# Storing the edge features once and splitting them on TensorE, in a four-layer graph network

## The reference, cut to what matters

```
edge_emb = edge_attr @ W_edge + b_edge
msg = jax.nn.relu(node_feats[src] + edge_emb)
aggr = jax.ops.segment_sum(msg, dst, num_segments=N)
h = (1.0 + eps) * node_feats + aggr
```

## Time and profile before

| what | value |
|---|---|
| time, median of 3 runs (lowest to highest) | 3059.01 us (3057.54 to 3060.01) |
| profiled execution, first to last instruction | 2795.5 us |
| mean granted TensorE clock | 0.952 |
| PE busy, share of the span | 2528.3 us, 90% |
| DVE busy | 2138.1 us, 76% |
| ACT busy | 1682.1 us, 60% |
| POOL busy | 1299.1 us, 46% |
| DMA moved | 338.46 MB |

### The profile page before, as it was taken

One profiled execution on the slowest core, in us unless ns is written; L12 is line 12 of the kernel. 1 busy time (PEld: TensorE's weight loads), 2 busy tenths in 40 slices (PEclk: granted clock), 3 DMA queues, 4 the chain that ended last, 5 costly groups with the idle time before them and its releaser, 6 DMA issues. The chain is left out here.

```text
span 2795.5 us, 45377 instructions
## 1 busy us (share of the span) xinstructions
PE 2528.3 (90%) x13039; PEld 1993.9 (71%) x13039; DVE 2138.1 (76%) x4172; ACT 1682.1 (60%) x3746; POOL 1299.1 (46%) x1279
## 2 busy tenths in 40 slices
PE   6999899999799999879899989598999999987887
PEld 4598555554488999648799984366888888765766
DVE  9699899998537888553588874866999999866667
ACT  1299888872226777413477761324888888845560
POOL 1777000007305677640377667315777777710211
PEclk9999999999899999998999999899999999988999
DMA  2210000013344453324455447225888888840201
GB/s 90 78 40 3 13 0 0 0 43 123 124 179 121 145 147 112 124 76 158 112 149 140 146 107 91 98 89 188 276 276 278 274 273 278 232 104 32 78 1 45
DMA packets 126768, 338.46 MB, mean 121 GB/s; under 512 B 25255, under 2 KB 39530, under 8 KB 126638
## 3 DMA queue, kind: packets, MB, share of 16 engines
q0 software_dynamic: 60768, 172.88, 22.0%
q1 hardware_dynamic: 65870, 163.93, 18.0%
HBM read 243.04 MB, written 85.82 MB: 118 GB/s over the span
## 5 line engine op out<-in xcount | busy, mean ns | idle before, releaser
L1839 POOL DMA_INDIRECT x_got<-table_dram,src_idx x376 | 418.8, 1114 | 117.3 <-issue 99.3
L722 POOL DMA_INDIRECT feature_rows<-in_edge_attr,ids x376 | 367.4, 977 | 117.4 <-issue 110.1
L1969 DVE TENSOR_TENSOR msg<-bank,x_got 128x512 f32<-128x512 f32 x376 | 252.7, 683 | 73.6 <-PE bank L1864 53.5
L1278 DVE TENSOR_TENSOR pt_low<-bank,pt_high 128x640 fp32r<-128x640 f32 x320 | 262.8, 822 | 54.9 <-ACT pt_high L1241 53.4
L673 ACT ACTIVATE hot_rest<-hot_dst,slot_w 128x128 bf16<-128x128 bf16 x864 | 272.6, 399 | 38.4 <-DVE hot_dst L633 38.4
L1241 ACT CAST pt_high<-bank 128x640 fp32r<-128x640 f32 x320 | 219.9, 688 | 117.6 <-PE bank L1192 117.4
L725 POOL COPY ids<-id_idx 128x136 uint32<-128x136 uint32 (+2 forms) x5 | 1.2, 242 | 612.5 <-DVE id_idx L840 347.6
L1918 ACT ACTIVATE msg_high<-msg 128x512 fp32r<-128x512 f32 x329 | 206.8, 628 | 74.8 <-DVE msg L1969 74.8
L1272 DVE CUSTOM_DVE_ANT_0 p<-bank,log_counts 128x1254 f32<-128x1254 f32 x160 | 232.6, 1454 | 13.7 <-PE bank L1175 13.6
L1192 PE MATMUL bank<-ident,p 128*128 128x128 f32 x1600 | 229.1, 275 | 2.3 <-DVE pt_low L1278 2.3
L1949 DVE SCALAR_TENSOR_TENSOR msg_low<-msg,msg_high 128x512 fp32r<-128x512 f32 x329 | 223.7, 680 | 0.0
(11 more groups left out here) (408 smaller groups left out, 6687.9 us busy)
## 6 DMA issues: line engine op xcount, KB each, us to landing
features_dram<-feature_parts POOLq DMA_DIRECT2D x94, 512.0 KB, 3.0
edge_got<-features_dram SPq DMA_DIRECT2D x94, 512.0 KB, 4.9
qk_dram<-qk_high SPq DMA_DIRECT2D x16, 640.0 KB, 2.9
qk_dram<-qk_low SPq DMA_DIRECT2D x16, 640.0 KB, 4.2
keys<-qk_dram SPq DMA_DIRECT2D x32, 320.0 KB, 4.7
queries<-qk_dram SPq DMA_DIRECT2D x32, 320.0 KB, 6.7
queries_low<-qk_dram SPq DMA_DIRECT2D x32, 320.0 KB, 8.9
acc_a<-zeros SPq DMA_DIRECT2D x1, 6400.0 KB, 30.6
```

Source lines behind the costliest of these rows:

```text
L722: pool.indirect_dma_start(out=rows[:, g % 2, j * ED:(j + 1) * ED], out_offset=None, in_=self.a.edge_attr_128, in_offset=bass.IndirectOffse ...
L1278: dve.tensor_tensor(p_low[:, made % 3, :, columns], unit(2 * n + u).rearrange("p (j n) -> p j n", n=P), p_high[:, made % 3, :, columns].bi ...
L1839: pool.indirect_dma_start(out=xg[:, g % XRING, j, :], out_offset=None, in_=k.table_dram, in_offset=bass.IndirectOffsetOnAxis(ap=k.src_idx[ ...
L1969: dve.tensor_tensor(msg[:, j, :], k.bank[:, 2 + j, :], xg[:, r, j, :], ALU.add).then_inc(added_x, 1)
```

## The change

The features are stored whole. POOL only gathers and saves: the float32r copy, the subtraction and `parts` are gone, the save (now 256 KB) goes straight out of `rows[:, u]`, and therefore the gathers of group g+1 now stand behind the wait for the save of group g-1, whose buffer they overwrite.

In `edge_messages`, PE turns four whole float32 tiles in transpose mode into one bank (bank 0 for even groups, 1 for odd). ACT copies the bank to float32r, which is the high part. PE then adds a product of minus the identity with that high part into the same bank (`take_off`), which leaves the low part there, and ACT copies the bank a second time. So the split of a group is a chain turn, high copy, `take_off`, low copy. PE does `take_off` behind the following `embed`; ACT does the high copy early, right behind the first rectification and the one-hot matrix of group g, and the low copy behind all of them.

```diff
@@ Features.gather @@
         for g in range(first, first + groups):
             u = g % 2
+            if g > first:
+                gate(pool, self.saved, of(16 * g, 16 * LAYER_GROUPS), self.passed)
             if g + 1 < first + groups:
                 load(g + 1)
             gate(pool, self.got[u], of(16 * GT * (g // 2 + 1), 16 * GT * LAYER_GROUPS // 2), self.passed)
-            if g > first:
-                gate(pool, self.saved, of(16 * g, 16 * LAYER_GROUPS), self.passed)
-            pool.tensor_copy(parts[:, 0, :], rows[:, u, :]).then_inc(self.made, 1)
-            gate(pool, self.made, of(2 * g + 1, 2 * LAYER_GROUPS), self.passed)
-            pool.tensor_tensor(parts[:, 1, :], rows[:, u, :], parts[:, 0, :].bitcast(F32), ALU.subtract).then_inc(self.made, 1)
-            gate(pool, self.made, of(2 * g + 2, 2 * LAYER_GROUPS), self.passed)
-            pool.dma_start(k.features_dram[bass.ds(of(g, LAYER_GROUPS), 1), :, :].rearrange("g p n -> (g p) n"),
-                           parts[:].rearrange("p q n -> p (q n)").bitcast(F32)).then_inc(self.saved, 16)
+            pool.dma_start(k.features_dram[bass.ds(of(g, LAYER_GROUPS), 1), :, :].rearrange("g p n -> (g p) n"), rows[:, u, :]).then_inc(self.saved, 16)
@@ layer2 @@
-            dve.tensor_copy(messages.ident_r[:], k.ident[:]).then_inc(messages.w_split, 1)
+            dve.tensor_scalar(messages.minus_r[:], k.ident[:], -1.0, None, ALU.mult).then_inc(messages.w_split, 1)
@@ edge_messages, PE @@
                 if not first:
-                    pe.wait_ge(e_copied, (i * 2 + u) * 2)
+                    pe.wait_ge(e_low, i * 2 + u - 1)
                 pe.wait_ge(got_e[u], i * 16 + 16)
-                for q in range(2):
-                    for j in range(GT):
-                        t = pe.matmul(k.bank[:, q, j * P:(j + 1) * P], ea[:, u, q, j, :], ident_r[:], start=True, stop=True)
-                    t.then_inc(turned_e, 1)
+                for j in range(GT):
+                    t = pe.matmul(k.bank[:, u, j * P:(j + 1) * P], ea[:, u, j, :], k.ident[:], is_transpose=True, start=(j == 0), stop=False,
+                                  skip_group_check=True)
+                t.then_inc(turned_e, 1)
+
+            def take_off(i, u):
+                pe.wait_ge(e_high, i * 2 + u + 1)
+                pe.matmul(k.bank[:, u, :], minus_r[:], et[:, u, 0, :], start=False, stop=True, skip_group_check=True).then_inc(e_rest, 1)
@@ the loop of pairs @@
                 turn(i + 1, 0)
                 embed(i, 1)
+                take_off(i + 1, 0)
                 collect(i, 0)
                 turn(i + 1, 1)
                 embed(i + 1, 0)
+                take_off(i + 1, 1)
                 collect(i, 1)
@@ edge_messages, ACT @@
                     if j == 0:
                         act.wait_ge(apart, g * GT + GT)
                         act.activation(hot[:, u], distance[:, u], ACT.Relu, bias=one[:], scale=-1.0).then_inc(hot_ready, 1)
+                        if following:
+                            copy_high(*following)
...
-                relu(i, 0)
-                copy_turned(i + 1, 0)
-                relu(i, 1)
-                copy_turned(i + 1, 1)
+                relu(i, 0, following=(i + 1, 0))
+                copy_low(i + 1, 0)
+                relu(i, 1, following=(i + 1, 1))
+                copy_low(i + 1, 1)
```

More of the change, by code:

```diff
@@ L704, in __init__ @@
         self.k, self.a = k, a
-        self.staged, self.made, self.passed = S("ids_staged"), S("parts_made"), S("features_passed")
+        self.staged, self.passed = S("ids_staged"), S("features_passed")
         self.got, self.saved = [S(f"features_got{u}") for u in range(2)], S("features_saved")
@@ L710, in places @@
         self.rows = r.take("feature_rows" + where, [P, 2, GT * ED], F32)
-        self.parts = r.take("feature_parts" + where, [P, 2, GT * ED], F32R)
     def gather(self, pool, first, groups, turn, l=None):
-        k, ids, rows, parts = self.k, self.ids, self.rows, self.parts
+        k, ids, rows = self.k, self.ids, self.rows
         def of(n, a_layer):
@@ L1530, in message_weights @@
     r = Region(nc, k.tail - 4 * KC * NP, k.tail)
[L1531 removed]
+    m.ea = r.take("edge_got", [P, 2, GT, ED], F32)
     m.we = r.take("w_edge", [ED, D], F32)
     m.w_high, m.w_low = r.take("w_edge_high", [ED, D], F32R), r.take("w_edge_low", [ED, D], F32R)
[L1534 removed]
+    m.minus_r = r.take("minus_ident_r", [P, P], F32R)
     m.one, m.one_eps = r.take("one", [P, 1], F32), r.take("one_eps", [P, 1], F32)
@@ L1813, in edge_messages @@
     xg = r.take("x_got", [P, XRING, GT, D], F32)
-    ea, w_high, w_low, ident_r, one = messages.ea, messages.w_high, messages.w_low, messages.ident_r, messages.one
+    ea, w_high, w_low, minus_r, one = messages.ea, messages.w_high, messages.w_low, messages.minus_r, messages.one
     et = r.take("edge_turned", [P, 2, 2, GT * P], F32R)
@@ L1882, in _ @@
             turn(0, 0, True)
-            turn(0, 1)
+            take_off(0, 0)
+            turn(0, 1, True)
+            take_off(0, 1)
             embed(0, 0)
@@ L1897, in _, with copy_high @@
         def _(act):
-            def copy_turned(i, u, first=False):
+            def copy_high(i, u, first=False):
                 g = i * 2 + u
@@ L1902, in copy_turned, with copy_low, relu @@
                     act.wait_ge(emb_done, (g - 1) * GT)
-                for q in range(2):
-                    act.wait_ge(turned_e, g * 2 + q + 1)
-                    act.copy(et[:, u, q, :], k.bank[:, q, :]).then_inc(e_copied, 1)
+                act.wait_ge(turned_e, g + 1)
+                act.copy(et[:, u, 0, :], k.bank[:, u, :]).then_inc(e_high, 1)
+            def copy_low(i, u):
+                g = i * 2 + u
+                act.wait_ge(e_rest, g + 1)
+                act.copy(et[:, u, 1, :], k.bank[:, u, :]).then_inc(e_low, 1)
             def apart_from(g, u, j):
                 act.activation(distance[:, u, j, :], k.row128f[:], ACT.Abs, bias=k.slot_dst[:, bass.ds(g * GT + j, 1)], scale=-1.0).then_inc(apart, 1)
-            def relu(i, u, first=False, last=False):
+            def relu(i, u, first=False, last=False, following=None):
                 g = i * 2 + u
```

24 lines of the change are left out of this document (13 added, 11 removed).

## The result

On the chip of the first measurement the changed kernel took 3087.64 us (median of 6 runs, 3078.91 to 3109.17) against 3059.51 for the kernel before: ratio 1.0099, 95% interval 1.0072 to 1.0126. The forecast was 3039, range 3020 to 3060. Its own profiled execution took 3081.72 us with a span of 3079.7.

The account below looks back on a forecast made before the run. The prediction took PE to bound the message loop and POOL to set the end of both attends. Message loop −16, attends −2 and finish_layer scaling −2 gave −20 us, 3059 to 3039, range 3020 to 3060.

Parts of the forecast that it names:

- Sum: Whole kernel: span 2795.5 to 2775.5, −20; the median, 263.5 above the span, moves by the same, 3059 to 3039.
- A: Message loop: PE's cheaper turn, less one added product, saves .37 us a pair over 43 pairs: −16, from −21 to −8.
- B: Ends of both attends: POOL loses its compute but waits openly for saves: −2 us together, from −9.5 to +20.
- C: finish_layer: DVE's scaling no longer meets POOL's operations, so a few get shorter: −2 us, from −4 to 0.
- collision: Attends: a save meeting query and key loads, landing about 6 us; one for each of seven later heads, +11 to +17.
- a landing of 2.25: Attends: issue to landing of a 256 KB save, 3.00 for 512 KB less .75 of data; bounds 1.5 to 3.00.
- Rival 3: Message loop: the early high copy holds ACT, making the kernel slower, about 3100 us; chance .10.
- a chain over 5.71 us: Message loop, turn to turn: 4.6 us without hand-overs, taken as 5.0; over 5.71 a group the kernel gets slower.
- first hand-over: Message loop: one of four passings between engines on the chain, each taken at .1 us, with .3 surely above it.
- Rival 1: Attends: POOL is later because save landings are fully exposed: 3059 us, range 3041 to 3066; chance .15.

Follow-up runs that it names:

- c0_before: The kernel before, unchanged, run again with a profile on another chip than the first measurement's: 2792.05 us, ratio 1.0003.
- c6_before: The kernel before, unchanged, one run for a trace beside c5_after: 2786.43 us.
- c5_after: The changed kernel, unchanged, on a chip where the kernel before took 2793.67 us: 2774.85 us, ratio 0.9938.
- e3_inc: The changed kernel with the loop's turn signal given by the first product of the following embed: 2790.09 us, ratio 0.9997.
- e4_late: The changed kernel with ACT's high copy moved behind all four rectifications: 2774.25 us, ratio 0.9943.
- c7_before: The kernel before, unchanged, with a trace on a chip of the slower kind, where it takes 3045 to 3060 us: 3058.83 us.
- c9_after: The changed kernel, unchanged, once more on a chip where the kernel before took 3047 us: ratio 0.9972.
- e8_few_gathers: The changed kernel, but POOL gathers only the first two groups of each block's share and saves those buffers repeatedly: ratio 0.9859.
- e10_pauses: The changed kernel with three row buffers, high copy behind the third rectification, and a waited-for POOL memset behind each feature gather: ratio 0.9872.
- e13_pauses: The kernel of e10_pauses run again, on a chip where the kernel before took 3045 us: ratio 0.9889.
- e14_pauses: The kernel of e10_pauses once more, on a chip where the kernel before took 3047.48 us: ratio 0.9878.
- e7b_ring3_j2: The changed kernel with three row buffers and the high copy behind the third rectification, without pauses: 3294.46 us, ratio 1.0776.
- e15_ring3_j2: The kernel of e7b_ring3_j2 once more, where the kernel before took 3058.96 us: ratio 1.0786.

## Why the prediction was wrong

**The step that failed** is under *Sum*: "The median of the runs lies 263.5 above the span; none of the changed work is there, so it moves by the same." The 263.5 us were inside the span of the timed executions: 2.0 us lie outside it (3081.72 less 3079.7), and the rest is in sorting (169), the loop (80) and the attends (16) of an S chip. The changed work stands in the last two of these. The trace that was read and the times that were forecast came from chips of two kinds. A program whose span is 9% short of its time should have been doubted, not carried over.

Between the two S traces (c7_before and the first profile after) the −16 of A became +10, the −2 of B +19 and the −2 of C −9; with −2 in sorting and tail, +19 in all. The medians differ by 28: the profiled execution after was 6 us faster than its median, that of before 3 slower.

Its own steps hold for the most part on the kind of chip whose trace they read (c0_before, c6_before and c5_after): predicted −20, measured −18.8.

- *A, message loop, −16 (−21 to −8):* 560.7 and 560.4 to 546.1, −14.4. The turn took .41 for .38, `take_off` .23 for .24, ACT's wait .76 us a group (69.0 in 91), just within the .8 given.
- *B, attends, −2 (−9.5 to +20):* the attends of the two profiles of before, 312.8 and 311.5 on average, to 308.7 and 315.2: −4.1 and +3.7, together −.4. That close a hit is luck: with e3_inc and e4_late, whose attends have the same code, the mean after is 312.8 and 317.0, together +5. The group without a collision was forecast at 7.9 and took 7.89, by two errors that cancel: the open wait was 2.5 to 2.6 for a landing of 2.25, and .3 ahead of the first gather went into the wait. From issue to landing the profiles have 3.0 for 512 KB and 2.4 for 256 KB as medians, so halving the save took away .6, not the .75 of the prediction. The Trainium skill ("DMA: Bandwidth & Descriptors", anatomy of one DMA, GpSimd path), by its sum of 2.0 us and the bytes at 436 GB/s, leads to an estimated 3.2 and 2.6, the same .6; the trace agrees here within .2.
- *C, −2:* the scaling takes .930 in the middle and .966 at most, where it was 1.857 at most. Layer 0 and the two finishing blocks came out 2.4 and 2.8 shorter and 2.0 longer than the mean of before's two profiles, −3.2 in all; that the scaling did this was not tried apart.

**On an S chip** none of the rivals names what happened. Rival 3, the early high copy holding ACT, is the nearest, and its place is right: ACT stood at the turn for 149.6 us in the loop, DVE's low parts and PE's collect behind it. But its cause, a chain over 5.71 us, is not there: where the signal comes on time the chain holds. What failed in the chain is its first hand-over, from turn to high copy, taken at .1: it is .23 on time (.64 less the turn's .41) and over .7 in 29 of 91 waits. Rival 1 gave a POOL that is later in the attends; in the first profile after, POOL's last save was issued at 1320.33 and the block ended at 1347.26, so POOL was early and the attention itself was slow. How POOL's gathers stand in time did change: before, each row of four was followed by 2.7 us of compute; after, by an open wait of 2.5 and more. That this made the attends 10 us longer is not shown, and c9_after, with the same rows, has attends of 319.

**Shown:** that the S chip's loss sits in three stretches in which POOL issues rows of indirect DMAs (c7_before), while layer 0, which has such rows too, loses nothing; that in an attend it goes away with the gathers (e8_few_gathers) and all but goes with a pause behind each (e10_pauses, e13_pauses, e14_pauses); that without any pause it grows to 130 us an attend (e7b_ring3_j2 and e15_ring3_j2). **Argued, not shown:** that the turns of the message loop are late by the same cause; the times of POOL's last gathers speak for it, but a loop with real pauses or fewer gathers was not run. **Open:** why one chip does this and another doesn't, and why PE stands; whether the distance or the number of gathers counts; why the changed kernel loses 1.0% on one S chip and gains .3% on another (attends 331 and 319, loop 651 and 625, with 29 and 35 late turns); what pauses cost on an F chip. No version was found that was tried on both kinds and is best on both: the changed kernel with three buffers and the copy behind the third rectification has 0.985 on F and 1.078 on S; with pauses 0.987 to 0.989 on S; with two buffers 0.994 on S.

## What to carry to other kernels

Before a difference in a span is carried over to a time, see that span and time belong together: a gap of more than a few us between them is a question about the chip, not a constant. A wait or a computation that separates an engine's DMA issues may be doing work that no view shows; where a change takes it away, look at what the other engines get done per 100 us while the issues run. And a copy that feeds a product in the same bank is best placed where neither engine has to stand for it. On an F chip with three buffers that was behind the third of four operations: a loop of 536 us against 547 and 544 at the two ends. On S chips the place told nothing: 620 to 626 behind the third, 624, 625 and 651 behind the first.

## What the runs showed of the hardware

- The same program took 2790 us on two chips and 3045 to 3060 on others. In the stretch from 100 to 200 us PE executed 413 products at a granted clock of 0.97 on the one kind and 42 at 0.53 on the other, POOL being busy for 77 us with indirect DMAs on both. The gaps came first: PE stood for 2.21 us at a clock of 1.00 before the clock fell to 0.50.
- Gathers of 0.95 us with .30 between them, 69 in 100 us, went with 197 products of PE on an S chip where 696 were done with POOL idle; with 1.02 between them, 47 in 100 us, it was 701. In layer 0 the same gathers cost PE nothing (135 products in 50 us on both kinds).
- The signal of a product was seen up to 4.8 us, and once 18.1, behind the product's start where .64 is usual, by ACT and SP at once, and in 16 of 29 cases .86 to 1.7 us after POOL's gathers had paused.
- A DMA from POOL took 3.0 us from issue to landing for 512 KB and 2.4 for 256 KB (medians of before and c5_after).
